# Gate parts of the expert loop in 32-row blocks, gate matmuls of blocks 0 and 1 in two row groups of the array

## The reference

```python
z = jnp.einsum('nd,sdr->nsr', xf, P)              # S = 8 blocks, R = 16
scores = jnp.einsum('nsr,smr->nsm', z, C)         # M = 64 experts per block
topv, topi = jax.lax.top_k(scores, 4)
w = jax.nn.softmax(topv, axis=-1)
h = gelu(einsum('nsr,nskrh->nskh', z, W1[s, topi]) + b1[s, topi])    # 32 hidden
yl = einsum('nskh,nskhr->nskr', h, W2[s, topi]) + b2[s, topi]
comb = jnp.einsum('nskr,nsk->nsr', yl, w)
out = gelu(comb.reshape(N, 128) @ G1 + g1b) @ G2 + g2b
```

## Time and profile before

| | us |
|---|---|
| median of 3 runs | 971.04 |
| lowest, highest | 970.57, 973.81 |
| the profiled execution, its time | 974.09 |
| its span, first to last instruction | 972.3 |
| PE busy in the span | 899.8 |
| DVE busy | 671.3 |
| ACT busy | 593.7 |
| POOL busy | 477.6 |

### The profile page before, as it was taken

How to read it: one execution, slowest core, us unless ns; L and a number is a source line. 1 busy time by engine, 2 the same in 40 slices (tenths; PEclk the granted TensorE clock), 3 DMA queues, 4 the chain that set the end, 5 groups by cost and what they waited for, 6 DMA issues and landing times.

```text
span 972.3 us, 16073 instructions
## 1 busy us (share of the span) xinstructions
PE 899.8 (93%) x5394; PEld 417.3 (43%) x5394; DVE 671.3 (69%) x1670; ACT 593.7 (61%) x870; POOL 477.6 (49%) x446
## 2 busy tenths in 40 slices
PE   3599999999999978799999999999999999999997
PEld 1267777777777756222222322322232223222322
DVE  4346555666666667677777888787777877876764
ACT  0221211125332245688888889898889888987774
POOL 0133434233335525477755666556556655664442
PEclk8699999999999977799999999999999999999999
DMA  9300001000000176766778787879788878888672
GB/s 269 118 1 1 1 2 69 2 1 1 1 1 15 30 129 97 227 204 213 220 221 248 229 243 239 249 226 247 213 250 232 254 208 243 235 246 276 231 235 97
DMA packets 87212, 151.32 MB, mean 156 GB/s; under 512 B 30083, under 2 KB 54276, under 8 KB 86481
## 3 DMA queue, kind: packets, MB, share of 16 engines
q1 hardware_dynamic: 86158, 147.04, 50.8%
q10 hardware_dynamic: 972, 3.24, 2.6%
HBM read 135.99 MB, written 14.25 MB: 155 GB/s over the span
## 4 chain that ended last, share of the span: by engine, by line
PE 78%; ACT 10%; DVE 5%; issue 2%; DMA 1%; SPq 1%; POOL 1%; ACTq 0%; DVEq 0%; POOLq 0%
PE ps L760 17%; PE ps L699 14%; PE ps L737 8%; PE ps L422 8%; PE ps L430 5%; PE ps L489 4%; PE ps L481 3%; PE ps L498 3%; PE ps L539 2%; PE ps L459 2%; ACT ring L1057 2%; PE ps L511 2%; ACT L939 2%; DVE ring L1494 1%; ACT ring L1064 1%
## 5 line engine op out<-in xcount | busy, mean ns | idle before, releaser
L1696 POOL TENSOR_TENSOR ring<-ring,wbc 128x512 f32<-128x512 f32 x192 | 244.7, 1279 | 170.4 <-ACT ring L1064 162.4
L1494 DVE TENSOR_TENSOR ring<-ps,ring 128x1024 f32<-128x1024 f32 x192 | 235.0, 1224 | 109.4 <-PE ps L737 80.1
L699 PE MATMUL ps<-zst,w1st 99*128 99x512 bf16 x768 | 216.0, 388 | 18.0 <-ACT ring L1057 14.2
L760 PE MATMUL ps<-ring,w2cur 128*32 128x512 f32 x1536 | 205.6, 608 | 0.0
L1057 ACT ACTIVATE ring<-ps 128x1024 f32<-128x1024 f32 x192 | 197.2, 1027 | 6.4 <-PE ps L699 6.1
L1551 POOL TENSOR_TENSOR t<-t 128x768 f32<-128x768 f32 x48 | 87.4, 1832 | 204.4 <-DVE t L1185 204.4
L1066 ACT ACTIVATE ps<-ps 128x512 f32<-128x512 f32 x192 | 113.9, 593 | 59.2 <-PE ps L699 59.2
L699 PEld LDWEIGHTS ps<-zst,w1st 99*128 99x128 bf16 x768 | 72.0, 98 | 156.5 <-ACT ring L1057 34.6
L1497 DVE TENSOR_TENSOR ring<-ps,wbc 128x512 f32<-128x512 f32 x192 | 130.5, 680 | 1.4 <-DMA wbc<-w_rows 1.4
L737 PE MATMUL ps<-wst,sel 96*128 96x512 bf16 x384 | 119.0, 392 | 6.3 <-DVE ring L1494 5.4
L1183 DVE TENSOR_TENSOR t<-ps,rope 128x768 f32<-128x768 f32 x48 | 45.7, 952 | 110.1 <-PE ps L430 73.9
(11 more groups left out here) (166 smaller groups left out, 1149.5 us busy)
## 6 DMA issues: line engine op xcount, KB each, us to landing
wbc<-w_rows SPq DMA_DIRECT2D x192, 512.0 KB, 5.2
w2cur<-in_w SPq DMA_DIRECT2D x48, 256.0 KB, 4.6
w_parts<-wp SPq DMA_DIRECT2D x72, 64.0 KB, 3.3
zst<-z_parts SPq DMA_DIRECT2D x72, 64.0 KB, 5.1
wst<-w_parts SPq DMA_DIRECT2D x72, 64.0 KB, 4.6
w1st<-w_parts ACTq DMA_DIRECT2D x12, 256.0 KB
z_parts<-zp SPq DMA_DIRECT2D x6, 384.0 KB, 5.2
out_h<-h SPq DMA_DIRECT2D x12, 192.0 KB, 4.5
```

What stands on the lines that cost most here:

```text
L699: return pe.matmul(bank(to), w1st[0:99, 4 * a + j, col:col + P], zst[0:99, (i // 2) % 2, j, :], start=True, stop=True)
L760: mm = pe.matmul(bank(YBANK, 0, 512, 32 * j, 32 * j + 32), w2cur[:, n, j, :], ring[:, (4 * g + j) % RING, :], start=False, stop=(n == 7 an ...
L1494: dve.tensor_tensor(v, ps[:, WBANK * 512:WBANK * 512 + 1024], v, ALU.mult).then_inc(s["duo_done"], 1)
L1696: pool.tensor_tensor(ring[:, slot, :], ring[:, slot, :], wbc[:, g % 4, 1, :], ALU.mult).then_inc(s["tri_done"], 1)
```

## The change

The gate parts are interleaved: 32 rows now hold eight experts, each with its three parts and a row of zeros (r, m, k with k = 4). `sel` is [128, 2, 128]: each group of 32 rows has the same matrix, for the lower and the upper four of the eight experts. The group n needs only the 32-row block n//2. The matrices of j = 0 lie in `wst` in their order and those of j = 1 are rotated by 32 rows, so that for each n the two matmuls read different row groups. The zero rows are filled once by a DMA from an input of zeros. `sel` is loaded as bf16 bits straight into place, and ACT's cast is gone.

```diff
-    w_parts = nc.dram_tensor("w_parts", (3, S * M // 2, B * T), BF16, kind="Internal").ap()
+    w_parts = nc.dram_tensor("w_parts", (2, 2, 2, 4, 8, 4, B * T), BF16, kind="Internal").ap()
...
-            sel = alloc(region, "sel", [96, 8, P], BF16)
-            sel_f = ring[0:96, 0:2, :]
+            sel = alloc(region, "sel", [P, 2, P], BF16)
...
+            sp.dma_start(w_parts[:, :, :, :, :, 3, :].rearrange("a j t r m n -> (a j t r m) n").bitcast(F32),
+                         t["zeros"].to_broadcast([S * M // 2, B * T // 2])).then_inc(s["zeroed"], 16)
             sp.wait_ge(s["w1_lo"], 1)
...
-                    sp.dma_start(w_parts[k, :, tile * P:tile * P + P].rearrange("(g p) n -> p g n", p=P),
+                    sp.dma_start(w_parts[:, :, :, :, :, k, tile * P:tile * P + P].rearrange("g j t r m n -> (j t r m) g n"),
                                  wp[:, k, :, :]).then_inc(s["w_stored"], 16)
...
-                for k in range(3):
-                    row = w_parts[k, a * P:a * P + P, blk * BLK:blk * BLK + BLK]
-                    sp.dma_start(wst[32 * k:32 * k + 32, i % 2, :, :],
-                                 row.rearrange("(j e m) n -> e m j n", j=2, e=2)[kt]).then_inc(s["wst_ld"], 16)
+                v = [w_parts[a, j, kt, :, :, :, blk * BLK:blk * BLK + BLK].rearrange("r m k n -> (r m k) n") for j in range(2)]
+                sp.dma_start(wst[:, i % 2, 0, :], v[0]).then_inc(s["wst_ld"], 16)
+                sp.dma_start(wst[32:P, i % 2, 1, :], v[1][0:96, :]).then_inc(s["wst_ld"], 16)
+                sp.dma_start(wst[0:32, i % 2, 1, :], v[1][96:P, :]).then_inc(s["wst_ld"], 16)
...
-            sp.dma_start(sel_f, t["sel"]).then_inc(s["ld_sel"], 16)
+            sp.dma_start(sel[:, :, :].rearrange("p q n -> p (q n)").bitcast(F32), t["sel"]).then_inc(s["ld_sel"], 16)
...
             load_z(0)
+            sp.wait_ge(s["zeroed"], 16)
             load_gates(0)
...
-                    mm = pe.matmul(bank(WBANK + j), sel[:, n, :], wst[0:96, i % 2, j, :], start=True, stop=True)
+                    q = 32 * ((n // 2 + j) % 4)
+                    mm = pe.matmul(bank(WBANK + j), sel[q:q + 32, n % 2, :], wst[q:q + 32, i % 2, j, :],
+                                   start=True, stop=True)
...
-            act.wait_ge(s["ld_sel"], 16)
-            act.copy(sel[:, :, :].rearrange("p q n -> p (q n)"), sel_f.rearrange("p a n -> p (a n)")).then_inc(s["sel_cast"], 1)
...
-    sel = np.zeros((3, 32, 8, 4, HID))
-    for m in range(32):
-        sel[:, m, m // 4, m % 4, :] = 1
+    sel = np.zeros((4, 32, 2, 4, HID), np.uint16)
+    for m in range(8):
+        sel[:, 4 * m:4 * m + 3, m // 4, m % 4, :] = 0x3F80
```

More of the change, by code:

```diff
@@ L178, in fused_layer @@
         block = ctx.enter_context(nc.Block())
-        names = ("ld_img ld_text ld_attn ld_mid ld_late ld_sel ld_w1 ld_scr0 ld_scr1 st_w1 st_z hot seen picked_s pix_t pixt_s img image "
+        names = ("zeroed ld_img ld_text ld_attn ld_mid ld_late ld_sel ld_w1 ld_scr0 ld_scr1 st_w1 st_z hot seen picked_s pix_t pixt_s img image "
                  "st1 st2 ln_var ln_std ln_done xn_d xn_t xn_e "
@@ L184, in fused_layer @@
                  "w_stored r_stored zst_ld wst_ld spread0 spread1 spread2 spread3 w2_lo w2_hi s_full s_copied t_full wT_done "
-                 "t_top t_mr p_dist e_done n_done p_em p_w hi_done r_done mid_done lo_done sel_cast "
+                 "t_top t_mr p_dist e_done n_done p_em p_w hi_done r_done mid_done lo_done "
                  "duo_full duo_gelu duo_w duo_done two_full two_gelu two_done tri_full tri_gelu tri_done "
@@ L689, in _ @@
             pe.wait_ge(s["x2_e"], 6)
-            pe.wait_ge(s["sel_cast"], 1)
+            pe.wait_ge(s["ld_sel"], 16)
             pe.wait_ge(s["ld_late"], 16 * 5)
@@ L1048, in final_gelu @@
                                bias=g1b[:, 0:1]).then_inc(s["u_done"], 1)
-            act.wait_ge(s["sel_cast"], 1)
             copy_scores(LEAD, PBANK)
@@ L1755, in constants @@
             "causal": np.triu(np.ones((P, P))).astype(f), "ident": np.eye(P, dtype=f),
-            "sel": sel.reshape(96, 2, BLK).astype(f), "halves": halves.astype(f),
-            "iota_p": np.arange(P, dtype=f)[:, None], "iota_x": np.tile(np.arange(IMG, dtype=f), (P, 1)),
+            "sel": sel.reshape(P, 2 * P).view(f), "halves": halves.astype(f),
+            "zeros": np.zeros((1, B * T // 2), f), "iota_p": np.arange(P, dtype=f)[:, None], "iota_x": np.tile(np.arange(IMG, dtype=f), (P, 1)),
             "ones": np.full((3, 2048), 0x3F803F80, dtype=np.uint32).view(f)}
```

## The result

The kernel after took 959.45 us (median of 4 runs, 957.64 to 961.78) against 971.00 for the kernel before: ratio 0.9876, 95% interval 0.9844 to 0.9909. A second set, side by side on one chip, gave 957.65 (6 runs) against 972.75: ratio 0.9849, interval 0.9817 to 0.9882. The forecast was 956.5, faster, with 951 to 961 as its own range. The direction was right, and so was the mechanism of the pair: the overlap and the price of one more change of shape. The size came out right in part by luck, because three terms of the sum were wrong and partly cancel: the gain at the boundaries and the number of pairs that pay were too high, and what was set aside for VectorE was too high as well.

What follows compares the result with a forecast made beforehand. The prediction took TensorE (PE), busy 93% of the span, as the bound. Its terms, 2.3 + 15.1 - 0.6 + 0.8 - 2.7 = 14.9, rounded to 14.5 us, gave 956.5 us; own range 951 to 961, with rivals 946 to 967.

Steps and rivals of the forecast that it cites:

- Part 1, the overlap: Gate pair: two 32-row matmuls in different row groups and banks run together, 0.33 us instead of 0.54.
- Part 2, one more change of shape: Behind the gate pair, going from the 32-row shape to the whole array costs 0.10 us, leaving 0.12 saved.
- Part 3, an ordinary pair where PE alone is the limit: Gate pair on the chain: each saves 0.12 us, and steady late groups take 2.28 us instead of 2.40.
- Part 3, the number of ordinary pairs: On the chain that ended last, 126 ordinary gate pairs save 0.12 us each, 15.1 us in all.
- Part 3, the boundaries: Start of each two iterations, 11 times: DVE starts one pass (0.21 us) sooner, 2.3 us in all.
- Part 3, given back to DVE: Groups with selection work, 18 iterations: DVE has no room, so 0.12 us per iteration is lost, 2.2 us in all.
- Part 3, the half-clock start: Start of the loop at 1.2 GHz, where a pass costs twice as much: about two pairs, 0.8 us gained.
- Part 4, the transfers: Wider gate loads, zero fill and smaller select matrix: hidden, counted as nothing; late DMA share rises to about 0.97.
- rival 2: Another engine or the DMA queues take over, above all in late groups: 4.8 us gained, 966 us; chance 0.15.
- The clock: Expected sign in the trace after the change: clock drops at three to five places.
- The sum: All gains and losses over the kernel: 2.3 + 15.1 - 0.6 + 0.8 - 2.7 = 14.9, rounded to 14.5 us.

Runs made afterwards that it cites:

- e2: Kernel after, but both gate matmuls of a pair read the same 32-row group, so they can't run side by side: 985.17 us, ratio 1.0141 to before.
- e11: Kernel before, with ACT's copy of the summed outputs cut to 64 of 512 columns: 972.08 us, ratio 1.0000 to before.
- e1: Kernel after's new data path alone, with each gate matmul still contracting all 128 rows, one after the other: 971.57 us, ratio 1.0006 to before.

## Why the prediction was right, point by point

- **Part 1, the overlap: right.** Two bf16 matmuls of 32 rows into two banks run side by side at the full rate, 3 ns apart (0.006 us for the f32 pairs). Worth 0.213 us a group by e2.
- **Part 2, one more change of shape: right.** 0.10 taken, 0.098 measured by e2 against the kernel before. The Trainium skill's rule in TensorEngine Tiling (Array Packing), Key Properties, that changing the tiling mode drains the engine, agrees; these runs add the price. The net of both, 0.12 forecast, was 0.115.
- **Part 3, an ordinary pair where PE alone is the limit: right.** In the late iteration without a boundary 8 x 0.115 = 0.92 was due and 0.90 came.
- **Part 3, the number of ordinary pairs: too high, and the largest error.** 126 pairs were counted from L737's share of the chain, some 90 of them (about 11 us) in the middle iterations. A piece on the chain pays in full only where no other chain is close behind it. In groups 3 to 6, 72 of the 144 middle groups, ACT was level with PE, and they gave 0.8 us in all. The prediction had seen that ACT's tables come due with PE, but set aside only 0.5 us for it.
- **Part 3, the boundaries: a step that failed.** The prediction gave each 0.21, since DVE starts one pass sooner. Late, a boundary gave 0.78 - 6 x 0.115 = 0.09. In the even iterations with selection the third group got 0.07 longer and the fourth 0.03. In its place stood a chain that the prediction did not look for: ACT's copy of the sums, placed ahead of two gelus, with DVE's L1498 behind. Before, cutting it changed nothing (e11), so it was the shorter of the two there. In the middle iterations ACT's tables stand behind it as well.
- **Part 3, given back to DVE: mis-sized.** 2.2 us were set aside for DVE's lag. Taking the selection work away gives 0.04 us in odd iterations and 0.01 in even ones, under 0.5 us in all. It shows (0.11) only once ACT's copy is short too, because the two chains end together. What was set aside too much here (about 2 us) makes up for part of what was counted too high in the two points before: the eighteen middle iterations were forecast at 15.1 + 2.3 - 0.6 - 2.7 less some 4.4 for the late part, 9.7, and gave 7.5. That the sum was no further off is luck.
- **Part 3, the half-clock start: right,** 0.71 against 0.8.
- **Part 4, the transfers: right.** e1 shows 0, but for the last step of `sel`. The zero fill landed 10.8 us after its issue and SP then still waited 125.5 us for the w1 parts. The DMA share in the late stretch went to 0.94 at 285 GB/s, not 0.97, and no wait of L1498 for `wbc` appeared there: rival 2 did not come.
- **The clock.** "Drops at three to five places" was wrong for the loop behind its start: one, but 6.8 us long. It cost 3.1 us where the three before had cost 4.1 together.
- **The sum.** The terms add up to 14.9, which was put down as 14.5 without a reason. 14.5 us were forecast and the medians gave 11.6 and 15.1 in two sets; the traces, with the clock drops taken out, gave 12.0 in the loop.

## What to carry to other kernels

When a contraction is short, cut it to 32 rows, place the operands of successive matmuls in different row groups and their outputs in different banks, and two of them ran as one here. But count the changes of array shape around them: here one more change (0.10) ate almost half of the pass saved (0.213). Don't take a line's share of the chain for what a cheaper line will pay: look in each stretch at how long the other engines have been idle, since the saving ends where one of them has no idle time left. And where an engine's release comes earlier by x, look for the second chain into the same waiter before booking x; if two end nearly together, experiments that remove one of them show little (0.01 and 0.13 here), and only the pair of removals shows the whole (0.24).

## What the runs showed that was not expected

- The price of a change of array shape was nearly the same, 0.09 to 0.11 us, in the cases read here: whole array to 32-column tiles, those to 32-row tiles, 32-row tiles to the whole array.
- The weight loads of the two row groups also run at once (both within 0.09 us).
- A drop of the granted clock to 0.50 (1.2 GHz) in the pause of the tables returned in the same iteration in both profiles of the kernel after, lasted 6.8 us and cost about 3 us; in the kernel before it lasted 3.4 us in three other pauses and cost 1.1 to 1.6 each. What decides which pause gets it was not found.
- A small copy of DVE (L1335 before) took 0.18 us in most iterations and 0.70 where it began 6 to 11 ns behind a tensor operation of POOL (L1604), ending just behind it. In e2, where it began 0.1 us behind, it took 0.60. So a few ns decide over half a microsecond, and which iterations get it changed from kernel to kernel. Why the copy waits was not tested.
